# Stage six of an eight-stage kernel: the weighted sum of a pair of units placed directly behind the scores of odd units, and ScalarE's exponentials placed ahead of its copies there

## The reference, cut to what matters

```python
xn = layer_norm(x, g_x, b_x)
ln = layer_norm(latents, g_l, b_l)
q = ln @ Wq                                   # (2, 1024, 16*64)
k, v = split(concatenate([xn, ln], axis=1) @ Wkv, 2)   # 77 + 1024 = 1101 keys
sim = einsum('bhid,bhjd->bhij', q * 64**-0.5, k)
attn = softmax(sim, axis=-1)
out = einsum('bhij,bhjd->bhid', attn, v)
out = layer_norm(out.reshape(b, 1024, 1024) @ Wout, g_o, b_o)
x = x + tanh(g_xattn[3]) * out
```

## Time and profile before

| | before |
|---|---|
| median of 3 runs (lowest to highest) | 2306.05 us (2305.68 to 2307.14) |
| the profiled execution's own time | 2320.85 us |
| its span in the trace | 2319.0 us |
| TensorE matmul busy | 2138.4 us (92% of the span) |
| VectorE busy | 1390.3 us (60%) |
| ScalarE busy | 1030.6 us (44%) |
| stage six's 128 iterations of scores | from 1108.03 us of the span to about 2189 us |

### The profile page before, as it was taken

One profiled execution on the slowest core, in us unless ns is written; L12 is line 12 of the kernel. 1 busy time (PEld: TensorE's weight loads), 2 busy tenths in 40 slices (PEclk: granted clock), 3 DMA queues, 4 the chain that ended last, 5 costly groups with the idle time before them and its releaser, 6 DMA issues. The chain is left out here.

```text
span 2319.0 us, 34530 instructions
## 1 busy us (share of the span) xinstructions
PE 2138.4 (92%) x13157; PEld 1519.3 (66%) x13157; DVE 1390.3 (60%) x3046; ACT 1030.6 (44%) x2153; POOL 129.3 (6%) x122
## 2 busy tenths in 40 slices
PE   6996997968999799796999999999999999999988
PEld 4875996434999688555566666666666666666643
DVE  5763112672444678687576666666566666666555
ACT  5752442530112522487444445444444444544455
POOL 1002111005122000000100000000000000000000
PEclk8997999889999999898999999999999999999999
DMA  3605996024897600200000000000000000000001
GB/s 117 173 3 174 310 324 231 19 79 133 270 318 260 197 1 1 78 1 9 4 1 1 1 1 1 1 1 1 1 1 1 1 1 1 1 1 1 1 1 36
DMA packets 109262, 159.78 MB, mean 69 GB/s; under 512 B 12555, under 2 KB 85165, under 8 KB 109101
## 3 DMA queue, kind: packets, MB, share of 16 engines
q1 hardware_dynamic: 101805, 134.80, 17.7%
q0 software_dynamic: 7296, 22.78, 2.9%
HBM read 127.64 MB, written 29.91 MB: 68 GB/s over the span
## 5 line engine op out<-in xcount | busy, mean ns | idle before, releaser
L608 PE MATMUL ps<-arena,w_odd 128*128 128x128 f32 (+4 forms) x2352 | 437.3, 439 | 3.0 <-DVE arena L2149 1.2
L608 PE MATMUL ps<-arena 128*64 128x256 f32 (+4 forms) x3216 | 388.2, 371 | 8.3 <-DVE arena L2280 4.5
L2470 DVE TENSOR_REDUCE small<-ps 128x1 f32<-128x1024 f32 x256 | 312.5, 1221 | 86.5 <-PE ps L608 86.5
L1717 ACT ACTIVATE arena<-ps 128x512 f32<-128x512 f32 x256 | 139.1, 594 | 452.8 <-PE ps L1171 452.7
L608 PEld LDWEIGHTS ps<-arena 128*64 128x64 f32 (+4 forms) x3216 | 254.5, 154 | 120.1 <-issue 22.6
L608 PEld LDWEIGHTS ps<-arena,w_odd 128*128 128x128 f32 (+3 forms) x2352 | 245.9, 187 | 106.0 <-issue 100.8
L1728 ACT ACTIVATE w_odd<-ps,small 128x1101 f32<-128x1101 f32 x256 | 302.7, 1183 | 6.5 <-DVE small L2471 4.7
L1171 PEld LDWEIGHTS ps<-ident,w_odd 128*128 128x128 f32 x2048 | 223.1, 141 | 121.0 <-issue 110.4
L1171 PE MATMUL ps<-ident,w_odd 128*128 128x128 f32 x2048 | 281.6, 277 | 9.5 <-DVE arena L2411 3.1
L2492 DVE COPY arena<-ps 128x512 f32<-128x512 f32 x256 | 164.3, 683 | 4.1 <-PE ps L1171 1.7
L608 PE MATMUL ps<-xn_feat,w_even 128*128 128x512 f32 (+1 forms) x352 | 137.9, 523 | 5.1 <-DVE xn_feat L2393 2.3
(11 more groups left out here) (386 smaller groups left out, 2928.8 us busy)
## 6 DMA issues: line engine op xcount, KB each, us to landing
w_odd<-in_s_w SPq DMA_DIRECT2D x32, 1024.0 KB
w_odd<-in_s_wgu SPq DMA_DIRECT2D x30, 704.0 KB
w_even<-in_s_w SPq DMA_DIRECT2D x15, 1024.0 KB
arena<-expert_rows_in SPq DMA_DIRECT2D x62, 130.0 KB
w_odd<-in_s_wd SPq DMA_DIRECT2D x30, 256.0 KB
out_feat<-in_s_wgu SPq DMA_DIRECT2D x10, 704.0 KB, 4.2
expert_rows_in<-zero_row POOLq DMA_DIRECT2D x1, 5070.0 KB, 32.5
vo_rows<-w_odd SPq DMA_DIRECT2D x8, 616.0 KB
```

The source lines that it names most:

```text
L608: return pe.matmul(o, lhsT, rhs, start=start, stop=stop, **kw)
L1717: act.activation(s6_pt[g % 2][0][:, 4 * i:4 * i + 4, c0:c0 + P], PS[:, bank, :].rearrange("p (a n) -> p a n", a=4), ACT.Copy).then_inc(r6_ ...
L2470: link(dve.tensor_reduce(m, s6_main[h], AX.X, ALU.max, negate=True))
```

## The change

On TensorE `weigh` moves from behind the pieces to directly behind the scores. The numbering list moves its output "v" to the front of the odd iteration. On ScalarE the two copies become a function; even iterations call it where it stood, odd iterations behind the two exponentials. VectorE's code isn't touched. No instruction is added or removed.

```diff
         for u in range(NU + 5):
             even = u % 2 == 0
             turn = 1 <= u <= NU
-            batch = [("p", u - 1, 0), ("p", u - 1, 1)] if turn else []
+            batch = [("v", (u - 3) // 2)] if not even and 3 <= u < NU + 3 else []
+            batch += [("p", u - 1, 0), ("p", u - 1, 1)] if turn else []
             if even and u // 8 < 15:
                 batch += [("w", u // 8 + 1, u % 8), ("w", u // 8 + 1, u % 8 + 1)]
-            if not even and 3 <= u < NU + 3:
-                batch += [("v", (u - 3) // 2)]
             batch += [("c", u - 1), ("p", u - 1, 2), ("p", u - 1, 3)] if turn else []
...
                     if u < NU:
                         scores(u)
+                    if not even and 3 <= u < NU + 3:
+                        weigh((u - 3) // 2)
                     if u == 0:
...
                             piece(n, i, free_bank(("w", n, i))).then_inc(r6_mm, 1)
-                    if not even and 3 <= u < NU + 3:
-                        weigh((u - 3) // 2)
                     if 1 <= u <= NU:
...
+                def p_copies(v):
+
+                    g, c0 = v // 2, (v % 2) * P
+                    for i in range(2):
+                        bank = filled(("p", v, i))
+                        act.activation(s6_pt[g % 2][0][:, 4 * i:4 * i + 4, c0:c0 + P], PS[:, bank, :].rearrange("p (a n) -> p a n", a=4), ACT.Copy).then_inc(r6_act, 1)
+
                 for u in range(NU + 5):
                     even = u % 2 == 0
                     n, j = u // 8 + 1, u % 8
-                    if 1 <= u <= NU:
-                        v = u - 1
-                        g, c0 = v // 2, (v % 2) * P
-                        for i in range(2):
-                            bank = filled(("p", v, i))
-                            act.activation(s6_pt[g % 2][0][:, 4 * i:4 * i + 4, c0:c0 + P], PS[:, bank, :].rearrange("p (a n) -> p a n", a=4), ACT.Copy).then_inc(r6_act, 1)
+                    if even and 1 <= u <= NU:
+                        p_copies(u - 1)
                     if u < NU:
...
                                 piece(n, j, filled(("w", n, j))).then_inc(r6_act, 1)
+                    if not even and u <= NU:
+                        p_copies(u - 1)
                     if even and 2 <= u <= NU:
```

## The result

| | before | after |
|---|---|---|
| median | 2306.6 us (4 runs) | 2328.61 us (4 runs) |
| lowest to highest | 2305.68 to 2308.84 | 2327.64 to 2329.30 |
| ratio, 95% interval | | 1.0094, 1.0081 to 1.0106 |
| the profiled execution, its span | 2320.85, 2319.0 | 2327.64, 2325.7 |

The changed kernel is 22.0 us slower; the forecast was 19.7, and 2328.6 us lies in the range of 2316 to 2335. The two profiled executions differ by only 6.8 us, because that of before entered stage six at 1108.03 us of its span and that of after at 1094.50: 13.5 us of the earlier stages, which the change does not touch. From the first scores of stage six to those of unit 127 the kernel before takes 1072.06 us and the changed one 1090.66, which is 18.6 more, and from there to the end 138.87 and 140.55, 1.7 more. Together 20.3 us.

What follows compares the result with a forecast made beforehand. TensorE's instruction list bounds stage six (busy 1052 of 1070 us). Losses of 12.0 us in 57 odd iterations, 6.2 in six behind a projection and 1.5 in iteration 1 make 2306.05 + 19.7 = 2325.8 us, range 2316 to 2335.

Steps and rivals of the forecast that it cites:

- The switch of shape: TensorE, odd iterations of stage six: one array-shape switch in and out fewer, 8.34 us instead of 8.49 without waits.
- direct switch: TensorE going straight from 64x128 scores to 128x64 weighted sum: priced like other switches, 0.15 us less or more possible.
- The banks: p2 and p3 in odd iterations wait for ScalarE's copies of p0 and p1: 0.36 us lost, 8.70 us in sum.
- the second wait: Within p2 and p3 of an odd iteration, for ScalarE's second copy: 0.08 us, beside 0.28 us ahead of p2.
- within 0.2%: Whole kernel: free switch (9.5 us less) and no second wait (5 less), giving 2311 us; chance 0.04.
- ScalarE: Normal odd iterations: ScalarE is free 0.57 us before p0's copy is due at 7.01 us, so its exponentials delay nothing.
- Six iterations behind a projection: Iterations 61, 63, 65, 67, 125, 127: copies wait for exponentials delayed by a table load, 1.04 us each, 6.2 together.
- Iteration 1: No weighted sum there; copies wait for the exponentials, so iteration 2 starts 1.54 us later.
- Sum: Whole kernel: 57 x 0.21 = 12.0, 6 x 1.04 = 6.2, and 1.5, together 19.7 us slower.
- The rival "faster": All 63 odd iterations: copies come in time, only the saved switch remains, 9.5 us less, 2296.6 us; chance 0.08.

Runs made afterwards that it cites:

- the run with c between them: Changed kernel with the context's transposes (c) between p2 and p3 in the 57 normal odd iterations: 2328.29 us, ratio 1.009.
- The run with a spare place for c: Changed kernel with the context's transposes (c) in unused columns of PSUM bank 2 in the 57 normal odd iterations: 2308.21 us, ratio 1.001.
- the old order in the seven: Changed kernel with c in spare bank 2 columns in 57 odd iterations, old order in iterations 1, 61, 63, 65, 67, 125, 127: 2298.21 us.

## Why the prediction was right

Point by point, by its own steps:

- *The switch of shape.* Foretold 0.15 us less per odd iteration, and a direct switch at the price of the others. Iteration 49 has the direct switch at the same 1.92 us, and with the bank wait removed the iteration is 8.34 us as foretold. Shown. The price of the direct switch had no row behind it, though: the prediction allowed 9.5 us either way for it, and that it came out in the middle is in part luck.
- *The banks.* Foretold 0.36 us and 8.70 us in sum, read from iteration 120, which had the same order of outputs. Measured 8.70 us, and taking c out of the rotation gives the 0.36 back. Shown. The prediction added a wait at p2 and a second at p3; the run with c between them shows that it is one bound, p1's copy, and not two that could be removed singly. In the rival "within 0.2%" I had the second wait go away by itself, which no run shows.
- *ScalarE.* Foretold an end of the exponentials 6.3 to 6.4 us into the iteration and copies at 7.01. Measured 6.44 (1506.61 and 0.19 more, against 1500.36) and 7.00. So ScalarE's order costs nothing in the 57, which its half alone shows too.
- *Six iterations behind a projection:* foretold 1.04 us each, measured 1.03. *Iteration 1:* foretold 1.54, measured 1.53.
- *Sum.* 19.7 us foretold, 20.3 in the traces, 22.0 in the medians, whose interval (18.7 to 24.4) holds all three. About 0.6 us of the trace's sum lies behind the scores of unit 127, beyond the 1.03 of that iteration, and was not looked into; from trace to trace that last part varies more (138.3 to 142.2 us). The medians' 1.7 us on top are within their noise.

The rival "faster" had the right gain per iteration and the wrong cover. Its price was wrong as well: 2296.6 us takes 0.15 off all 63 iterations and forgets the six behind a projection and iteration 1, where ScalarE is late whatever the banks do. The run with a spare place for c gives its condition to the other 57, and takes 2308.21 us; only with the old order in the seven is it 2298.21. The Trainium skill (TensorEngine Tiling (Array Packing), Key Properties) says that a change of tiling mode drains TensorE. The traces agree in that one change fewer saves 0.15 us per iteration (8.34 against 8.49). That sentence speaks of TensorE alone, and the loss came from the copies behind it.

## What to carry to other kernels

When outputs rotate through few banks, moving a long block changes which block covers the copies: here 4 us of weighted sum between p1 and p2 hid 1.1 us of copies, and moved ahead of p0 it hid none. Look for a place in the kernel before that already has the new order; iteration 120 gave the price of 57 others to a hundredth of a microsecond. And before removing one wait, ask which later wait ends at the same event: only another bank or another neighbour in the rotation, not a shift of the first wait, gave the time back (20.4 and 17.8 us of the 22.0, against 0.3).

## What the runs showed of the hardware

A wait of about two microseconds on TensorE can cost more than itself. In the run with TensorE's order alone, TensorE stands still ahead of iteration 50 (1.60 us by the records), and the iteration that follows takes 9.73 us instead of the 7.98 of the kernel before. Busy times and granted clock of iterations 49 and 50 of that run (the clock is the share of full speed behind POOL's busy time):

```profile
core 0: us, PE busy (x) PEld busy (x) DVE busy (x) ACT busy (x) POOL busy (x), PEclk, DMA share, GB/s
1557.70:1568.16 10.46, 8.74 (x67) 5.30 (x65) 6.08 (x13) 3.79 (x7) 0.00 (x0) 1.00 0.01 2
1568.16:1577.89 9.73, 9.51 (x47) 5.87 (x48) 5.30 (x11) 4.11 (x9) 0.00 (x0) 0.82 0.00 1
```

The granted clock is 0.82 over iteration 50, a mix of the two levels of 1.2 and 2.4 GHz, and the scores that follow the wait run at nearly half speed (3.37 us against 1.99). It doesn't happen behind every such wait. Of the 63 even iterations from 2 to 126 of that run, 34 have the lower clock in them. Iteration 46, behind the same wait, has not:

```profile
1531.66 0.53 PE L607 MATMUL ps<-w_even,w_odd 128*128 128x154 f32 x2 [1.60 <-ACT w_odd L1730]
1532.12 1.99 PE L607 MATMUL ps<-arena,w_odd 64*128 64x512 f32 x8
```

Nor is it scattered by chance: iterations 4, 28, 52, 76 and 100 have it, while 6, 30, 54, 78 and 102 take 7.00 us each, all of them behind the same wait. The kernel before has such a fall in iteration 126, behind a wait of 2.12 us, where the eight matmuls of the second row below take 2.63 us; the kernel with the old order in seven iterations has the same wait, 1.97 us for these eight and no fall:

```profile
2170.82 0.41 PE L1186 MATMUL ps<-ident,arena 128*128 128x128 f32 x2 [2.12 <-DVE arena L2489]
2171.42 2.63 PE L608 MATMUL ps<-w_even,xn_tok 128*128 128x256 f32 x8 [0.19 <-DVE arena L2492]
```

Iteration 126 of the two, the kernel before first:

```profile
2163.88:2180.09 16.21, 13.78 (x64) 10.37 (x63) 7.79 (x18) 5.18 (x8) 0.00 (x0) 0.89 0.01 1
2161.10:2175.60 14.50, 12.07 (x64) 9.19 (x63) 7.79 (x18) 5.18 (x8) 0.00 (x0) 1.00 0.00 1
```

16.21 us against 14.52. What decides it was not found. The waits of 0.3 us at p2 in the changed kernel don't bring it on: its even iterations from 2 on keep their times to a tenth of a microsecond. The sum of 20.3 us isn't touched by it either, since both of its traces have the fall in iterations 2 and 126.
